# Expert routing done pass by pass inside the main loop of a decoder layer, with feed-forward tiles loaded by address

## The chip, the cores and the metric

The kernel runs on one core of a Trainium2 chip. A core has the engines PE (TensorE: matrix products and transposes), DVE (VectorE), ACT (ScalarE), POOL (GpSimd) and SP (SyncE, which here only starts transfers), each with a queue of instructions of its own that is worked in order; they wait for each other by semaphores. The time is the device time of one execution in microseconds (us); lower is better.

## What is computed

The input x is 32 sequences of 128 tokens with 128 features. Three pre-normalised residual blocks follow each other: self attention that keeps the 32 largest scores of each row, cross attention with 16 heads of 8, and a feed-forward stage with 8 experts (128 to 512 to 128), of which each token uses one. The part that the change is about, cut from the reference:

```python
aff = feats @ centroids.T              # feats: 4096 tokens x 128, layernorm of x
eid = jnp.argmax(aff, axis=1)          # the expert of each token
xhat = (feats - mu) * jax.lax.rsqrt(var + EPS)
for e in range(E):
    mask = (eid == e)[:, None]
    h = xhat * gamma[e] + beta[e]
    y = feats + jax.nn.relu(h @ w1[e] + b1[e]) @ w2[e] + b2[e]
    alpha = jax.nn.sigmoid(feats @ centroids[e])[:, None]
    out = out + mask * (alpha * y + (1.0 - alpha) * feats)
x = x + out
```

## The kernel before

**Main loop.** The 32 sequences go in 8 groups (NG = 8) of 4 (G = 4). `passes` runs `run(g)` for g from -3 to 8 on every engine. Pass g does the cross attention of group g (`has_c`, g from 0 to 7), the second half of the self attention of group e = g + 2 (`has_e`), the first half of that of group h = g + 3 (`has_s`) and the features of group f = g - 1 (`has_f`), so that passes 1 to 4 carry all four, pass 5 has no h, passes 6 and 7 have neither e nor h, and pass 8 has only the features of group 7. Each pass is eight steps. The order inside a pass is written out by hand for each engine. DVE takes the maxima of the cross scores (`next_maxima`, L836; then `hmax_split`, L849 and L851), which PE transposes (L1266) before the scores can be shifted, exponentiated on ACT (L1058) and multiplied with the values (L1278). Between the maxima DVE does the normalisation of the heads (L858, L863), layernorm statistics (L607, L612, L614), the top-32 search (L824 MAX8, L828) and small steps of the features: `aff` is copied from PSUM (L995), its maximum taken (L1013), then 1/(1+exp(-max)) made (L1024, L1030).

POOL adds the attention result to the residual (`add_attended`, L695, on which DVE's statistics of the features wait), masks queries (L689), makes the reciprocal roots (L618, L775) and applies the norms (L622, L626), and makes the payload of a group, `pay`: per token 128 normalised features, 128 of x2 + feats, alpha (L779, L794), 260 words of 4 bytes in all. SP stores it to DRAM in token order (L585), one transfer of 520 KB per group. In passes 6 and 7 POOL also scales the first weights of 8 experts (`scale_w1`, L710), each after a product of PE (`expert_bias`, L1442) whose result DVE adds (L885).

**Routing.** After the last pass `route_vector` (L302 to L367) works on the affinities of all 4096 tokens at once: one-hot of the best expert, counts by two products of PE (L396, L397), a running sum, a slot for each token, and then the inverse of that map: ACT (L500, L504) and DVE (L350) build one-hot matrices, and 32 products of PE (L407) turn them into `gather_idx` and `scatter_idx`, a token number for each place of 39 tiles of 128 rows (each expert's tokens fill whole tiles).

**Feed-forward.** For each of the 39 tiles POOL gathers 128 rows of `pay` by an indirect transfer (L524) into a ring of RING = 6 buffers and scatters the result to the output by another (L528). PE transposes the tile (L421), multiplies with w1 of the tile's expert (L429) and w2 (L440); ACT copies the transposed rows (L481), copies w1 (L487) and takes relu (L493); DVE adds biases (L455, L463) and makes the result (L469). In POOL's queue the gather of tile t stands behind the wait for the result of tile t - 6, and the scatter of t - 6 behind that gather. The tile's expert number is read into a register by `expert_of` on PE, DVE and ACT.

## Time and profile before

| | us |
|---|---|
| median of 3 runs (485.59 to 493.64) | 487.68 |
| the profiled execution | 489.07 |
| its span, first to last instruction | 486.9 |
| PE busy | 376.5 |
| DVE busy | 310.1 |
| POOL busy | 253.6 |
| ACT busy | 238.3 |

The profile shows the execution that took 489.07 us; 2.2 us of it lie outside the span. Starts in the trace count from the start of the span. The span has three stretches: the main loop up to about 348 us, the routing up to 373 us, and the tiles up to the last scatter at 478 us, behind which only its landing and the end of the program lie. The chain that ended last has only that one transfer in it and so says nothing of the stretches; they are read from the instructions in order of time.

### The profile page before, as it was taken

What the parts mean: (1) busy time and instruction counts of PE and PEld (TensorE: products, weight loads), DVE (VectorE), ACT (ScalarE), POOL (GpSimd) and SP (SyncE); (2) the same over time, 40 slices, a digit from 0 to 9 for tenths busy, and PEclk for the clock granted to TensorE, in tenths of its full rate; (3) what the DMA queues carried; (4) which work ended last, traced back from release to release, by engine and by line L of the source; (5) the groups of instructions that cost most, each with busy time, mean ns of one, the idle gap of its engine ahead of it and who ended that gap; (6) DMA issues with size and microseconds to landing.
All of it is one profiled execution on the core that took longest, in us unless ns stands there. A gap on an engine that the chain in (4) does not pass through costs nothing. (4 is left out here: it accounts for less than half of the span.)

```text
span 486.9 us, 10893 instructions
## 1 busy us (share of the span) xinstructions
PE 376.5 (77%) x3453; PEld 245.1 (50%) x3454; DVE 310.1 (64%) x1194; ACT 238.3 (49%) x497; POOL 253.6 (52%) x319
## 2 busy tenths in 40 slices
PE   1757778978988988889898989897204988888870
PEld 1435424544544545545544545454204878778770
DVE  2376946697897897887878464452493545555550
ACT  1143613657666566666665534342043655555540
POOL 6933550135663863764647434444404477777771
PEclk9996955999999999999999799997555899999996
DMA  5010107500003001020011000100202132222220
GB/s 133 24 44 0 46 0 224 165 3 22 2 2 88 2 21 48 3 67 2 1 46 46 25 21 2 45 1 7 83 1 55 45 82 70 73 76 69 71 64 0
DMA packets 23949, 21.67 MB, mean 45 GB/s; under 512 B 3443, under 2 KB 20983, under 8 KB 23904
## 3 DMA queue, kind: packets, MB, share of 16 engines
q1 hardware_dynamic: 19488, 13.52, 9.3%
q0 software_dynamic: 3120, 7.30, 5.5%
q8 instruction: 25, 0.41, 0.4%
q10 hardware_dynamic: 1296, 0.28, 0.3%
q14 instruction: 20, 0.16, 0.1%
HBM read 14.73 MB, written 6.82 MB: 44 GB/s over the span
## 5 line engine op out<-in xcount | busy, mean ns | idle before, releaser
L836 DVE TENSOR_REDUCE neg_hmax<-s_bank 128x4 f32<-128x512 f32 x128 | 82.2, 684 | 49.8 <-PE s_bank L1242 49.5
L1058 ACT ACTIVATE weights<-s_bank 128x512 f32<-128x512 f32 x128 | 69.5, 595 | 70.3 <-PE s_bank L1258 64.1
L1242 PE MATMUL s_bank<-k_room,q_room 32*128 32x512 f32 x256 | 83.8, 669 | 3.2 <-DVE neg_hmax L836 3.2
L695 POOL TENSOR_TENSOR x<-x_bv,attended 128x128 f32<-128x128 f32 x32 | 14.6, 457 | 121.3 <-DVE attended L863 121.3
L1253 PE MATMUL s_bank<-q_room,k_room 32*128 32x512 f32 x256 | 73.9, 654 | 0.0
L524 POOL DMA_INDIRECT q_room<-routed_rows,gather_idx x39 | 38.2, 979 | 38.4 <-DVE scatter_idx L361 22.8
L1278 PE MATMUL pvt_bank<-weights,xv 128*32 128x128 f32 x1024 | 49.8, 288 | 10.3 <-ACT weights L1058 8.6
L455 DVE TENSOR_TENSOR q_room<-s_bank,b_cols 128x512 f32<-128x512 f32 x39 | 27.0, 691 | 41.5 <-PE s_bank L429 41.5
L528 POOL DMA_INDIRECT out<-x_in,scatter_idx x39 | 39.5, 1012 | 15.8 <-issue 12.5
L429 PE MATMUL s_bank<-k_room,self_room 128*128 128x128 f32 x312 | 44.5, 287 | 0.0
L1278 PEld LDWEIGHTS pvt_bank<-weights,xv 128*32 128x32 f32 x1024 | 21.7, 110 | 44.0 <-ACT weights L1058 40.5
L618 POOL TENSOR_TENSOR rstd<-var_eps,minus_half 128x4 f32<-128x4 f32 x24 | 24.4, 1018 | 32.2 <-DVE var_eps L614 31.5
L429 PEld LDWEIGHTS s_bank<-k_room,self_room 128*128 128x128 f32 x312 | 39.7, 199 | 0.4
L487 ACT ACTIVATE self_room<-w 128x512 f32 x39 | 24.6, 630 | 28.7 <-PE s_bank L429 23.9
L1258 PEld LDWEIGHTS s_bank<-hmax_t,head_sel 32*128 32x128 bf16 x512 | 20.4, 94 | 30.0 <-issue 28.5
L828 DVE MATCH_REPLACE8 self_room<-best,self_room 128x128 f32<-128x128 f32 x128 | 33.8, 274 | 0.0
L824 DVE MAX8 best<-self_room 128x8 f32<-128x128 f32 x128 | 27.6, 277 | 9.5 <-ACT self_room L1049 9.5
L493 ACT ACTIVATE q_room<-q_room 128x512 f32<-128x512 f32 x39 | 24.6, 630 | 12.5 <-DVE q_room L455 10.2
L1242 PEld LDWEIGHTS s_bank<-k_room,q_room 32*128 32x128 f32 x256 | 24.4, 190 | 9.4 <-issue 5.1
L421 PE MATMUL cross_bank<-ident,q_room 128*128 128x128 f32 x39 | 12.7, 326 | 18.5 <-DMA q_room<-routed_rows,gather_idx 18.4
L689 POOL TENSOR_SCALAR q_room<-q_room,head_mask 128x512 f32<-128x512 f32 x32 | 22.2, 695 | 8.3 <-ACT q_room L1051 8.3
L1258 PE MATMUL s_bank<-hmax_t,head_sel 32*128 32x128 bf16 x512 | 26.1, 218 | 0.0
(183 smaller groups left out, 783.8 us busy)
## 6 DMA issues: line engine op xcount, KB each, us to landing
routed_rows<-pay SPq DMA_DIRECT2D x8, 520.0 KB, 3.3
w<-in_w SPq DMA_DIRECT2D x16, 256.0 KB, 5.2
x_in<-in_x SPq DMA_DIRECT2D x8, 256.0 KB, 3.1
ctx_in<-in_ctx SPq DMA_DIRECT2D x8, 256.0 KB, 3.3
q_room<-routed_rows,gather_idx POOLq DMA_INDIRECT x39, 2.8
out<-x_in,scatter_idx POOLq DMA_INDIRECT x39, 2.3
x_in<-in_b SPq DMA_DIRECT2D x1, 512.0 KB, 4.8
xwk_t<-in_xwk_t ACTq DMA_DIRECT2D x1, 64.0 KB, 2.8
```

Source lines behind the costliest of these rows:

```text
L429: m = pe.matmul(s1_bank[:, (k % 2) * F + c * 128:(k % 2) * F + (c + 1) * 128], ffn_w1[k % 2][:, c * 128:(c + 1) * 128], ffn_row_t[k % 2], ...
L455: dve.tensor_tensor(by_chunk(ffn_hid[k % 2]), by_chunk(s1_bank[:, (k % 2) * F:(k % 2 + 1) * F]), spread(at(b1_cols, e * FC, FC).rearrange( ...
L524: pool.indirect_dma_start(out=ffn_row[k], out_offset=None, in_=rows, in_offset=bass.IndirectOffsetOnAxis(ap=gather_idx[:, t:t + 1].bitcast ...
L528: pool.indirect_dma_start(out=out_rows, out_offset=bass.IndirectOffsetOnAxis(ap=scatter_idx[:, old:old + 1].bitcast(U32), axis=0), in_=ffn ...
L824: dve.max(best8[:, b, r, :], at(src, b * S, S)).then_inc(s["topk_step"], 1)
L828: dve.match_replace(at(left, b * S, S), best8[:, b, r, :], at(src, b * S, S), TAKEN)\
L836: dve.tensor_reduce(neg_hmax[:, first:first + 4], bank.rearrange("p (h k) -> p h k", k=S), AX.X, ALU.max, negate=True).then_inc(s["s1_max" ...
L1058: act.activation(weights[:, u, :], s2_bank[:, (u % 2) * GS:(u % 2 + 1) * GS], ACT.Exp, scale=HEAD_SCALE).then_inc(s["s2_exp"], 1)
L1242: pe.matmul(s1_bank[:, (u % 2) * GS:(u % 2 + 1) * GS], natural(q_nat, g, j, strip(u)), masked(k_masked, g, j, strip(u)), start=True, stop= ...
L1253: pe.matmul(s2_bank[:, (u % 2) * GS:(u % 2 + 1) * GS], natural(k_nat, g, j, u), masked(q_masked, g, j, u), start=True, stop=False)
L1258: m = pe.matmul(s2_bank[:, (u % 2) * GS + i * S:(u % 2) * GS + (i + 1) * S], head_sel[32 * u:32 * (u + 1), i, :], hmax_t[32 * u:32 * (u + ...
L1278: m = pe.matmul(pvt_bank[32 * i:32 * (i + 1), (u % 2) * S:(u % 2 + 1) * S], xv[:, block:block + 32], weights[:, u, i * S:(i + 1) * S], sta ...
```

## The change

The routing is split over the passes. One pass after the affinities of a group, DVE marks the best expert of each token (`best_marked`, `best_ranked`, `first_best`: 4 operations of 128x32), PE counts (`count_rows`: 5 small bf16 products into a free part of `att_bank`), DVE reads the counts (`read_counts`) and makes a row number for each token (`slots`: 5 operations). Each expert has an area of its own in DRAM of CAP = 4224 rows, and POOL scatters the payload of a group straight into the areas (`scatter_rows`: 4 indirect transfers of 128 rows, 133 KB each), at four places of the pass for groups 0 to 5 (in pass f + 2), and all four behind each other at the end of pass f + 1 for groups 6 and 7. The payload gets two buffers and a token number in each row. SP's store of the payload is gone.

At the end `route_vector` only works out how many tiles each expert has and the first row of each tile (15 operations: 11 of 8 to 39 columns, 4 of 312). SP and ACT write a blank of 128 rows behind the end of each area (`blank_tails`, 8 transfers of 133 KB); the token number of a blank row is out of range, so that its result is not stored. SP then loads the 39 tiles with plain transfers at an address read from `tile_row` into a register (`ffn_sync`), up to eight ahead (RING = 8). POOL keeps only the scatter of the results, by the token numbers in the loaded rows. The products of L396, L397 and L407 and ACT's L500 and L504 are gone. `q_masked` is a ring of 2 in place of 3; POOL's wait for it then asks for the cross scores of group g - 1 in pass g.

```diff
-    NTC = NTILE + 1
+    CAP = B * S + 128
     PAY = 2 * D + 4
+    ALPHA, TOKEN = 2 * D, 2 * D + 1
+    NOWHERE = 1 << 20
...
-    RING = 6
-
-    rows = nc.dram_tensor("routed_rows", [B * S, PAY], F32, kind="Internal").ap()
+    RING = 8
+
+    rows = nc.dram_tensor("routed_rows", [E * CAP + 128, PAY], F32, kind="Internal").ap()
     out_rows = out.rearrange("b s d -> (b s) d")
...
+        Q_RING, K_RING = 2, 3
+        q_room = sb("q_room", [128, Q_RING * MASKED + 3 * GS])
+        k_room = sb("k_room", [128, K_RING * MASKED + 3 * GS])
+        q_masked, k_masked = q_room[:, 0:Q_RING * MASKED], k_room[:, 0:K_RING * MASKED]
+        q_nat, k_nat = q_room[:, Q_RING * MASKED:], k_room[:, K_RING * MASKED:]
...
+        def routed_at_once(f):
+
+            return f >= NG - 2
+
+        def routed_later(f):
+
+            return 0 <= f < NG - 2
...
+            dve.wait_ge(s["next_row_ready"], 1 + NG)
+            link(dve.tensor_scalar(next_row_i[:, :], next_row[:, :], 0.0, None, ALU.add))
+            s_ends = dve.tensor_scalar(first_f[:, 0:E], next_row[:, :], 127.0, None, ALU.add)
+            s_ends.then_inc(s["ends_ready"], 1)
+            dve.wait_ge(s["ends_ready"], 1)
+            link(dve.tensor_copy(tiles_i[:, :], first_f[:, 0:E]))
+            link(dve.tensor_scalar(tiles_i[:, :], tiles_i[:, :], 7, None, ALU.logical_shift_right))
+            link(dve.tensor_copy(tiles_of[:, :], tiles_i[:, :]))
+            link(dve.scalar_tensor_tensor(tiles_of[:, :], iota_f[:, 0:E], float(-CAP // 128), tiles_of[:, :], ALU.mult, ALU.add))
+            link(dve.tensor_tensor_scan(tiles_end[:, :], ones_f[:, :], tiles_of[:, :], 0.0, ALU.mult, ALU.add))
+            link(dve.tensor_scalar(jump[:, :], tiles_of[:, :], -128.0, float(CAP), ALU.mult, ALU.add))
+            link(dve.tensor_tensor(after[:, :, :], spread(col(iota_f[:, 0:NTILE]), [128, NTILE, E]),
+                                   spread(row(tiles_end[:, :]), [128, NTILE, E]), ALU.is_ge))
+            link(dve.tensor_reduce(expert_f[:, :], after[:, :, :], AX.X, ALU.add))
+            dve.tensor_scalar(tile_expert[:, :], expert_f[:, :], float(E - 1), None, ALU.min).then_inc(s["experts_ready"], 1)
+            link(dve.tensor_tensor(after[:, :, :], after[:, :, :], spread(row(jump[:, :]), [128, NTILE, E]), ALU.mult))
+            link(dve.tensor_reduce(first_f[:, :], after[:, :, :], AX.X, ALU.add))
+            link(dve.scalar_tensor_tensor(first_f[:, :], iota_f[:, 0:NTILE], 128.0, first_f[:, :], ALU.mult, ALU.add))
+            dve.tensor_scalar(tile_row[:, :], first_f[:, :], float(E * CAP), None, ALU.min).then_inc(s["tile_rows_ready"], 1)
             dve.wait_ge(s["experts_ready"], 1)
             ffn_vector(dve)
...
+            for t in range(NTILE):
+                k = t % RING
+                pool.wait_ge(s["result_ready"], t + 1)
+                pool.indirect_dma_start(out=out_rows,
+                                        out_offset=bass.IndirectOffsetOnAxis(ap=ffn_row[k][:, TOKEN:TOKEN + 1].bitcast(U32), axis=0),
+                                        in_=ffn_out[k], in_offset=None, bounds_check=B * S - 1,
+                                        oob_is_err=False).then_inc(row_scattered[k], 16)
             for k in range(RING):
                 n = len(range(k, NTILE, RING))
                 wait_alone(pool, row_scattered[k], 16 * n)
+
+        def blank_tails(eng, experts):
+            wait_alone(eng, s["route_step"], 1)
+            for e in experts:
+                end = eng.value_load(next_row_i[0:1, e:e + 1], min_val=0, max_val=E * CAP)
+                eng.dma_start(rows[ds(end, 128), :], blank[:, :]).then_inc(s["blanks_stored"], 16)
+
+        def ffn_sync(sp):
+            blank_tails(sp, range(0, E // 2))
+            wait_alone(sp, s["blanks_stored"], 16 * (1 + E))
+            for i in range(2):
+                wait_alone(sp, pay_stored[i], 16 * G * NG // 2)
+            wait_alone(sp, s["s2_done"], 4 * B)
+            wait_alone(sp, s["tile_rows_ready"], 1)
+            for t in range(NTILE):
+                k = t % RING
+                if t >= RING:
+                    wait_alone(sp, row_scattered[k], 16 * (t // RING))
+                first = sp.value_load(tile_row[0:1, t:t + 1], min_val=0, max_val=E * CAP)
+                sp.dma_start(ffn_row[k], rows[ds(first, 128), :]).then_inc(row_loaded[k], 16)
...
-                if has_f:
-                    wait_alone(sp, s["pay_ready"], g)
-                    wait_alone(sp, s["alpha_ready"], g)
-                    sp.dma_start(rows[ds((g - 1) * GS, GS), :].rearrange("(b s) c -> s b c", s=S),
-                                 pay[:, :, :]).then_inc(s["pay_stored"], 16)
...
+            def scatter_rows(f, j):
+
+                if j == 0:
+                    wait_alone(pool, s["pay_ready"], f + 1)
+                    wait_alone(pool, s["tokens_ready"], f + 1)
+                    wait_alone(pool, s["alpha_ready"], f + 1)
+                    wait_alone(pool, s["slots_ready"], f + 1)
+                at0 = half(f) * G + j
+                pool.indirect_dma_start(out=rows, out_offset=bass.IndirectOffsetOnAxis(ap=slot[:, at0:at0 + 1].bitcast(U32), axis=0),
+                                        in_=pay[:, at0, :], in_offset=None, bounds_check=E * CAP - 1,
+                                        oob_is_err=False).then_inc(pay_stored[half(f)], 16)
...
                         norm_apply(pool, 2, f, at(x2, half(f) * GS, GS), centred[:, :], feats[:, :], "feats_ready")
+                if routed_later(f - 1):
+                    scatter_rows(f - 1, 0)
...
+                    pool.iota(pay_of(f)[:, :, TOKEN].bitcast(I32), pattern=[[S, G]], base=f * GS, channel_multiplier=1)\
+                        .then_inc(s["tokens_ready"], 1)
+                if routed_later(f - 1):
+                    scatter_rows(f - 1, 3)
+                if has_f and routed_at_once(f):
+                    for j in range(G):
+                        scatter_rows(f, j)
...
+            def best_marked(f):
+
+                dve.wait_ge(s["aff_max_ready"], f + 1)
+                dve.tensor_tensor(chosen[:, :, :], aff[:, :, :], spread(col(aff_max[:, :]), [128, G, E]), ALU.is_equal)\
+                   .then_inc(s["chosen_step"], 1)
+
+            def best_ranked(f):
+
+                dve.wait_ge(s["chosen_step"], 3 * f + 1)
+                dve.tensor_tensor(chosen[:, :, :], chosen[:, :, :], spread(row(rank[:, :]), [128, G, E]), ALU.mult)\
+                   .then_inc(s["chosen_step"], 1)
+
+            def first_best(f):
+
+                dve.wait_ge(s["chosen_step"], 3 * f + 2)
+                dve.tensor_reduce(best[:, :], chosen[:, :, :], AX.X, ALU.max).then_inc(s["chosen_step"], 1)
+                dve.wait_ge(s["chosen_step"], 3 * f + 3)
+                dve.tensor_tensor(onehot[:, 0:G, :], chosen[:, :, :], spread(col(best[:, :]), [128, G, E]), ALU.is_equal)\
+                   .then_inc(s["onehot_ready"], 1)
+
+            def read_counts(f):
+
+                dve.wait_ge(s["counts_done"], f + 1)
+                dve.tensor_copy(counts[:, :, :], att_bank[:, COUNTS:COUNTS + (G + 1) * E].rearrange("p (b e) -> p b e", e=E))\
+                   .then_inc(s["counts_read"], 1)
+
+            def slots(f):
+
+                dve.wait_ge(s["counts_read"], f + 1)
+                dve.wait_ge(s["next_row_ready"], f + 1)
+                dve.tensor_tensor(placed[:, :, :], counts[:, 0:G, :], spread(row(next_row[:, :]), [128, G, E]), ALU.add)\
+                   .then_inc(s["placed_step"], 1)
+                dve.wait_ge(s["placed_step"], 3 * f + 1)
+                dve.tensor_tensor(next_row[:, :], next_row[:, :], counts[:, G, :], ALU.add).then_inc(s["next_row_ready"], 1)
+                dve.tensor_tensor(placed[:, :, :], placed[:, :, :], onehot[:, 0:G, :], ALU.mult).then_inc(s["placed_step"], 1)
+                dve.wait_ge(s["placed_step"], 3 * f + 2)
+                dve.tensor_reduce(slot_f[:, :], placed[:, :, :], AX.X, ALU.add).then_inc(s["placed_step"], 1)
+                if later(f, 2):
+                    dve.wait_ge(pay_stored[half(f)], 16 * G * (f // 2))
+                dve.wait_ge(s["placed_step"], 3 * f + 3)
+                dve.tensor_copy(slot[:, half(f) * G:(half(f) + 1) * G], slot_f[:, :]).then_inc(s["slots_ready"], 1)
...
                     next_maxima(g, 0, 2)
+                if routed_later(f - 1):
+                    read_counts(f - 1)
...
                 expert_bias(g, 0)
+                if routed_later(f - 1):
+                    slots(f - 1)
...
+                    best_marked(f)
                 if has_s:
-                    topk(h, 2)
+                    topk_best(h, 2)
+                if has_f:
+                    best_ranked(f)
+                if has_s:
+                    topk_take(h, 2)
+                if has_f:
+                    first_best(f)
 
                 if has_c:
                     next_maxima(g, 3, 2)
                 if has_s:
                     topk(h, 3)
+                if has_f and routed_at_once(f):
+                    read_counts(f)
+                    slots(f)
...
+                if j == 0 and routed_later(g - 2):
+                    pe.wait_ge(s["counts_read"], g - 1)
+                if j == 3 and routed_at_once(g - 1):
+                    pe.wait_ge(s["counts_read"], g)
...
+                def count_rows(of):
+                    pe.wait_ge(s["onehot_ready"], of + 1)
+                    pe.wait_ge(s["iota_made"], 5)
+                    pe.wait_ge(s["attended_ready"], G * (of + 2) if routed_later(of) else min(G * of + 7, B))
+                    pe.matmul(att_bank[:, COUNTS:COUNTS + (G + 1) * E], earlier[:, :],
+                              onehot[:, :, :].rearrange("p b e -> p (b e)"), start=True, stop=False)
+                    for b in range(G):
+                        m = pe.matmul(att_bank[:, COUNTS + (b + 1) * E:COUNTS + (G + 1) * E], all_ones[:, :],
+                                      spread(onehot[:, b:b + 1, :], [128, G - b, E]), start=False, stop=b == G - 1)
+                    m.then_inc(s["counts_done"], 1)
...
                         transposed(lambda b: xn[:, b * S:(b + 1) * S], self_bank, h, "xn_ready", h + 1, "xn_transposed")
+                    if routed_later(f - 1):
+                        count_rows(f - 1)
...
                         project(cross_bank, xwq_t, xn2_t, "xn2_t_ready", e + 1, "xq_done")
+                    if routed_at_once(f):
+                        count_rows(f)
```

## Rows read from the trace of the kernel before

**Rows 1.** Busy time by window: start:end, length, PE, PEld, DVE, ACT, POOL, PE's clock, DMA.
```profile
207.10:240.60 33.50, 30.09 (x336) 17.09 (x336) 28.53 (x119) 21.28 (x46) 19.99 (x25) 1.00 0.09 25
...
373.00:380.00 7.00, 6.31 (x28) 6.00 (x29) 1.38 (x2) 3.76 (x8) 3.33 (x4) 0.50 0.34 94
```
**Rows 2.** DVE in time, passes 4 and 5: start, us, line, operation, [idle before].
```profile
223.98 1.29 DVE L836 TENSOR_REDUCE neg_hmax<-s_bank 128x4 f32<-128x512 f32 x2 [0.81 <-PE s_bank L1242]
...
255.87 1.28 DVE L836 TENSOR_REDUCE neg_hmax<-s_bank 128x4 f32<-128x512 f32 x2
```
**Rows 3.** PE and its weight loads in time, start of pass 4.
```profile
217.61 0.10 PEld L1266 LDWEIGHTS s_bank<-ident_bf,hmax_parts 128*128 128x128 bf16 x1 [1.44 <-DVE hmax_parts L851]
...
220.02 0.66 PE L1217 MATMUL self_bank<-ident,self_room 128*128 128x128 f32 x4
```
**Rows 4.** POOL in time, between passes 3 and 4.
```profile
214.89 1.04 POOL L626 TENSOR_TENSOR self_room<-centred,rstd 128x512 f32<-128x512 f32 x1
218.13 0.46 POOL L695 TENSOR_TENSOR x<-x_bv,attended 128x128 f32<-128x128 f32 x1 [2.20 <-DVE attended L863]
```
**Rows 5.** Timeline: two DVE operations, and the POOL instruction beside each.
```profile
199.84 1.04 POOL L626 TENSOR_TENSOR xn<-centred,rstd 128x512 f32<-128x512 f32 x1
200.00 0.92 DVE L849 CAST hmax_parts<-neg_hmax 128x16 bf16<-128x16 f32 x1
...
369.74 1.24 POOL L524 DMA_INDIRECT q_room<-routed_rows,gather_idx  x1 [22.77 <-DVE scatter_idx L361]
370.10 0.18 DVE L366 TENSOR_SCALAR k_room<-k_room 128x40 f32<-128x40 f32 x1
```
**Rows 6.** Timeline of the last two passes.
```profile
338.66 1.04 POOL L794 TENSOR_TENSOR pay<-feats,rstd 128x512 f32<-128x512 f32 x1
339.66 0.45 POOL L695 TENSOR_TENSOR x<-x_bv,attended 128x128 f32<-128x128 f32 x1
...
347.62 0.19 DVE L995 COPY aff<-att_bank 128x32 f32<-128x32 f32 x1 [3.77 <-PE att_bank L1416]
```
**Rows 7.** Timeline of the routing.
```profile
352.43 0.40 PE L396 MATMUL s_bank<-k_room,earlier 128*128 128x256 bf16 x1 [4.85 <-DVE k_room L311]
...
353.08 0.69 DVE L313 COPY k_room<-s_bank 128x512 f32<-128x512 f32 x1 [0.70 <-PE s_bank L397]
...
356.32 0.17 DVE L325 TENSOR_TENSOR k_room<-k_room 128x8 f32<-128x8 f32 x1
356.52 0.17 DVE L326 SCALAR_TENSOR_TENSOR k_room<-k_room 128x8 f32<-128x8 f32 x1
...
369.06 0.48 DVE L363 TENSOR_TENSOR k_room<-iota_f,k_room 128x320 f32<-128x320 f32 x1
```
**Rows 8.** PE's tile transposes in time: tiles 0, 3, 6 and 38.
```profile
372.95 0.45 PE L421 MATMUL cross_bank<-ident,q_room 128*128 128x128 f32 x1 [5.06 <-DMA q_room<-routed_rows,gather_idx]
...
379.79 0.42 PE L421 MATMUL cross_bank<-ident,q_room 128*128 128x128 f32 x1
...
385.81 0.27 PE L421 MATMUL cross_bank<-ident,q_room 128*128 128x128 f32 x1
...
470.08 0.33 PE L421 MATMUL cross_bank<-ident,q_room 128*128 128x128 f32 x1 [0.58 <-DMA q_room<-routed_rows,gather_idx]
```
**Rows 9.** POOL's steady pace in the tiles, in time.
```profile
427.35 0.98 POOL L524 DMA_INDIRECT q_room<-routed_rows,gather_idx  x1 [0.30 <-issue]
...
428.63 1.01 POOL L528 DMA_INDIRECT out<-x_in,scatter_idx  x1 [0.30 <-issue]
```
**Rows 10.** The page, part 6: transfers, us from issue to landing.
```profile
q_room<-routed_rows,gather_idx POOLq DMA_INDIRECT x39, 2.8
out<-x_in,scatter_idx POOLq DMA_INDIRECT x39, 2.3
```
**Rows 11.** Timeline: a start by SP; ACT's copy of w1 behind a register read.
```profile
2.76 0.43 SPq L551 DMA_DIRECT2D bias_cols<-in_bk  x1
...
374.08 0.63 ACT L487 ACTIVATE self_room<-w 128x512 f32 x1 [0.37 <-issue]
```

269 lines of the change are left out of this document (83 added, 186 removed).

## The prediction

> **What bounds the kernel now.** I read the page first, then the busy time by window, then the waits, and last each stretch in order of time. The chain of waits on the page ends in one scatter and does not help, so each stretch has to be judged by itself.
>
> In the main loop a full pass takes 33.5 us, of which PE is busy 30.1, DVE 28.5 and POOL 20.0 [rows 1]. DVE has 119 instructions in it, and behind most a gap of some 0.04 us, 4 to 5 us in all, so DVE has nearly no idle time left. PE and DVE take turns: at one place PE waits 1.44 us for the split maxima [rows 3], at another DVE waits 0.81 us for PE's scores, and at the same place a pass later it waits for nothing [rows 2]. An operation added to DVE therefore costs between nothing and its whole length, by its place. POOL has 13 us to spare, mostly in waits for DVE; one of them is 2.20 us [rows 4].
>
> The routing lies bare: from the last copy of the affinities at 347.62 [rows 6] to the first transpose of a tile at 372.95 [rows 8] it takes 25.3 us, and neither PE nor POOL has other work.
>
> In the tiles two paces stand beside each other. POOL spends 0.98 + 0.30 + 1.01 + 0.30 = 2.59 us per tile on a gather and a scatter [rows 9]. PE, where it did not wait for rows, went from tile 3 to tile 6 in 385.81 - 379.79 = 6.02 us, 2.01 us per tile [rows 8]. The stage as a whole went from tile 3 to tile 38 in 90.3 us, 2.58 us per tile, so POOL sets it. The first three intervals are an exception: PE then had a granted clock of 0.50, the level of 1.2 GHz [rows 1], behind a stretch in which it had been nearly idle, and needed 379.79 - 372.95 = 6.84 us for them.
>
> **The change, part by part.**
>
> *Tiles.* POOL loses the gather and comes down to 1.01 + 0.30 = 1.31 us per tile. PE is next, at 2.01 us; I take 2.04, a little over it, because the three intervals are few. SP's own pace is not in the trace: a start took it 0.43 us, and a register read on ACT showed as at most 0.37 us of idle time before L487 [rows 11]. With a wait in front I estimate 1 us per tile, and up to eight tiles of lead. Its bounds are 0.43 us, the bare start, and 2.59 us, the nearest loop of starts and waits that there is [rows 9]; above 2.04 it would show. ACT and DVE kept up with the 2.01. A row load takes about what a gather took to land, 2.8 us [rows 10], against a lead of 8 x 2.04 = 16 us. So tiles 0 to 3 take 6.84 us as before, tiles 3 to 38 35 x 2.04 = 71.4, together 78.2 in place of 470.08 - 372.95 = 97.1: **-18.9 us**. What follows tile 38 stays, 486.9 - 470.08 = 16.8.
>
> *From the last affinities to the first tile.* Small dependent operations of DVE follow each other by 356.52 - 356.32 = 0.20 us [rows 7]. From the copy of `aff`: the maximum and four marking operations end at 0.2 + 5 x 0.2 = 1.25. The old counts took 353.08 - 352.43 = 0.65 us from PE's start to DVE's read [rows 7]; five products of at most 40 columns are taken the same, 1.9. `read_counts` and the five of `slots` make 3.1, two for alpha 3.5. Then three things run beside each other. (1) POOL issues four scatters: 1.24 for a first indirect transfer [rows 5], then 3 x 1.31, the last landing 2.3 us behind its start, at about 3.5 + 1.24 + 2.6 + 0.3 + 2.3 = 9.9. (2) DVE's end of the routing: 11 operations by 0.20 and four of 312 columns by 0.52 (0.48 [rows 7] and a gap), 4.3, ready at 7.8. (3) `next_row_i` at 3.7; SP and ACT then write four blanks each, a register read and a start, 0.43 to 1.2 us each, so that the last starts between 5 and 8.5 and lands some 3 later, at 8 to 11.5; I take 10.6. Then a register read, a start and 2.8 us of landing, 3.6 to 3.9: the first transpose at **14.5** in place of 25.3, a gain of 10.8 us; the bounds are 12 and 18.
>
> *POOL's queue at the end of pass 7.* Here the moved work falls on the path. Before, POOL ended `pay` (L794) at 339.70 and at 339.66 began the last addition to the residual (L695) [rows 6], on which the last group's statistics, its features and its affinities hang. The operand of that addition had come at 338.95. Now the token numbers (about 0.2), `scatter_rows(5, 3)` and the four of group 6 stand between the two: 5 x 1.28, by (0.98 + 0.30) of [rows 9], is 6.4. What waits is L695, and with it everything to the last affinities: **+6.6 us**, bounds 5 and 8. So little of the routing gain is left: 10.8 - 6.6 = **-4.2 us** at the start of the tiles.
>
> *Main loop.* DVE: four marking operations, two of them between independent ones, some 0.65 us, in passes 1 to 4 in a place where PE later waits for DVE [rows 3]: on the path, 4 x 0.65 = 2.6. `read_counts` and `slots`, six operations, 1.2 us, in passes 2 to 5, before the L836 that once had 0.81 us of idle time and once none [rows 2]: 0.7 each, 2.8. Passes 5 to 7 have less DVE work; five products of PE (0.3 to 0.6 us) in each cost a little there, together 0.1. Sum **+5.5 us**, bounds 1 (all hidden) and 12 (7 passes x (0.65 + 1.2) uncovered, less 1).
>
> POOL: four scatters by 1.28, 5.1 us per pass, into 13 us of idle time. The worst place is the end of a pass: two scatters and the token numbers, 2.7 us, ahead of `first_norm`, whose end at 215.93 [rows 4] goes to 218.6. PE takes those rows at 220.02 [rows 3], and the addition behind had 2.20 us of idle time. Hidden, by 1.4 us; that much more POOL time in this place would reach PE, and DVE's `read_counts` behind it.
>
> SP's store of 520 KB goes; its landing was hidden. The q ring of two asks for scores that POOL's own wait for the last head result already implies: nothing. At the start POOL loses three small constants and gains four: nothing.
>
> *Two engines at one memory.* A cast of 16 columns (L849) took 0.92 us, not about 0.17, beside an arithmetic instruction of POOL; L366 beside an indirect transfer on POOL took 0.18 [rows 5]. So I give the scatters no price on DVE. The Trainium skill, SBUF — State Buffer, section "Who interferes with whom", says that VectorE's two-port modes and GpSimd exclude each other for the whole instruction, whoever issues first, and that descriptor making suffers by this too. By that rule the cast of this trace is explained, and the scatters would meet DVE operations as well, which the pair with L366 does not show.
>
> **The sum.** -18.9 - 10.8 + 6.6 + 5.5 = -17.6 us. On the profiled execution 489.07 - 17.6 = 471.5. That execution lies 1.4 us above the median of 487.68, so for the median: 487.7 - 17.6 = **470 us**, 3.6% less.
>
> **The rivals.**
>
> 1. *The small work is hidden and the path at pass 7 is shorter.* Main loop +1 and the start at 12 in place of 14.5: 470 - 4.5 - 2.5 = 463; with POOL's stop at 5 us, 461. For it: passes 5 to 7 wait often on PE. Against: the places where PE waits for DVE.
> 2. *The tiles stop at another bound.* SP's wait, register read and start, or a chain over ACT and DVE, at 2.3 to 2.4 us per tile: 35 x 0.33 = 11.5 more, 481.5, within 2%. For it: SP's pace was never seen, and PE's was seen only on a few tiles. Against: [rows 11].
> 3. *The scatters disturb the loop.* If 24 scatters of groups 0 to 5 each hold DVE or are held as the cast was, 0.92 - 0.17 = 0.75 us, that is 18 us: 488, no change. The rule of the Trainium skill above, SBUF — State Buffer, goes this way. Half of it gives 479. Against: L366.
> 4. *Slower.* SP's loads come at a pace P. The forecast turns to a loss of over 2% (above 497.4) when 35 x (P - 2.04) passes 27.4 us, at P = 2.82 us per tile; at 3.0 the time is 504. Against it: even POOL, with two indirect transfers, needs 2.59.
>
> **How the numbers follow.** Forecast as told (465 to 476) 0.47, rival 1 0.15, rival 2 0.16, rival 3 0.14 (half of it near 479, half near 488), rival 4 0.05, other 0.03. About 2% is what a measurement of this kernel can tell from no change; faster means below 477.9. Faster: 0.47 + 0.15, a third of rivals 2 and 3, 0.72. Same: the rest of these, 0.21. Slower: rival 4, a little of the other, 0.07. The range reaches from rival 1 to rival 2 with half of rival 3: 459 to 485.
>
> **What would show it.** In the changed kernel: L421's successor every 2.0 to 2.1 us with clock 1.00 and no wait for a load behind the first; POOL busy about half of the tile stage; five indirect transfers in a row on POOL before the last L695, which starts 6 to 7 us behind L794's successor; 14 to 15 us from the last copy of `aff` to the first transpose; full passes 1 to 1.5 us longer; small DVE casts of 0.17 us beside scatters. The prediction is wrong if tiles come at over 2.2 us, if passes grow by over 2.5 us, or if L695 does not wait for the scatters.

## The result, and the profile after

| us | before | after |
|---|---|---|
| median of 20 runs each | 486.86 (484.99 to 493.64) | 483.22 (482.12 to 488.1) |
| the profiled execution, its span | 489.07, 486.9 | 483.1, 481.3 |
| PE, DVE, POOL, ACT busy | 376.5, 310.1, 253.6, 238.3 | 380.5, 318.9, 249.6, 229.7 |

The ratio of the runs is 0.995, with a 95% interval of 0.9932 to 0.9967. The change is worth 3.6 us where 17.6 were forecast. By the two spans it is 5.6 us; the profiled execution of before lay over the median of its kernel and that of after on it, which makes the other 2 us. In one group of experiments (the first section on them) the runs of before stood at 516.7 us, far from the 486 to 487 of all the other groups; no trace of such a run was kept, and the reason is open. The changed kernel was not timed in that group, so its kernels are set against the changed kernel's 483.0 to 483.2 of the others.

The span falls into the same stretches as before. Each difference below is between two rows of the same kind, of [rows 6] and [rows 8] for before and of the fences for after.

| stretch | before | after | difference | forecast |
|---|---|---|---|---|
| start to the end of the pass-7 payload (POOL) | 339.7 | 354.0 | +14.3 | +5.5 |
| from there to the last addition to the residual | 0.0 | 6.5 | +6.5 | +6.6 |
| last addition to the last copy of the affinities | 8.0 | 8.0 | 0.0 | 0 |
| last affinities to the first tile transpose | 25.3 | 14.8 | -10.5 | -10.8 |
| first to last tile transpose | 97.1 | 81.8 | -15.3 | -18.9 |
| last transpose to the end of the span | 16.8 | 16.2 | -0.6 | 0 |

The busy time by window of the kernel after (start:end, length, then PE, PEld, DVE, ACT, POOL, PE's clock, DMA share, GB/s). The first three are passes 1, 2 and 3, cut at the copies of `aff`; the last two are the tiles:

```profile
138.69:175.61 36.92, 32.75 (x341) 18.65 (x341) 30.94 (x138) 21.60 (x47) 22.01 (x28) 0.95 0.05 16
175.61:212.06 36.45, 33.06 (x341) 17.96 (x341) 32.08 (x139) 21.49 (x47) 24.64 (x31) 0.95 0.07 24
212.06:249.40 37.34, 32.97 (x341) 18.30 (x341) 31.77 (x130) 21.60 (x47) 24.62 (x31) 0.95 0.07 23
383.00:390.00 7.00, 6.08 (x27) 5.81 (x28) 1.38 (x2) 3.76 (x8) 0.00 (x0) 0.50 0.44 116
390.00:465.00 75.00, 72.80 (x596) 68.95 (x595) 46.48 (x105) 49.28 (x104) 32.98 (x35) 1.00 0.31 84
```

Cut in the same way, the three passes of before take 34.1, 34.1 and 33.7 us, so they grew by 2.8, 2.3 and 3.6; PE's mean clock in them is 0.95 and not 1.00. From the first copy of `aff` to that of pass 7 the loop took 189.7 us before and takes 203.5 after. A second profile of the changed kernel (`after_again`) has 206.9 there, so a difference of 3 us between two profiled loops is within what one kernel shows. In the tiles PE is busy 97% of the time at clock 1.00, and POOL 44%.

The end of pass 7 on POOL, and the last copy of `aff`, in order of time (start, us, engine, line, operation, [idle before]):

```profile
352.97 1.04 POOL L740 TENSOR_TENSOR pay<-feats,rstd 128x512 f32<-128x512 f32 x1
353.96 0.14 POOL L743 IOTA pay<- 128x4 int32 x1
354.26 1.07 POOL L634 DMA_INDIRECT routed_rows<-pay,slot  x1 [0.16 <-issue]
...
359.49 0.98 POOL L634 DMA_INDIRECT routed_rows<-pay,slot  x1 [0.30 <-issue]
360.49 0.47 POOL L623 TENSOR_TENSOR x<-x_bv,attended 128x128 f32<-128x128 f32 x1
...
368.48 0.19 DVE L1009 COPY aff<-att_bank 128x32 f32<-128x32 f32 x1 [3.77 <-PE att_bank L1445]
```

Five indirect transfers stand between the payload and the addition (L623, L695 before), as forecast: 360.49 - 354.0 = 6.5 us.

The start of the tiles: SP's four blanks, the last scatter, SP's first load, and the transposes of tiles 0, 3 and 38 on PE:

```profile
372.73 4.36 SPq L447 DMA_DIRECT2D routed_rows<-blank  x4
...
376.58 0.97 POOL L634 DMA_INDIRECT routed_rows<-pay,slot  x1 [0.30 <-issue]
...
381.16 0.36 SPq L461 DMA_DIRECT2D q_room<-routed_rows  x1
...
383.30 0.45 PE L351 MATMUL cross_bank<-ident,q_room 128*128 128x128 f32 x1 [13.15 <-DMA q_room<-routed_rows]
...
390.05 0.31 PE L351 MATMUL cross_bank<-ident,q_room 128*128 128x128 f32 x1
...
465.12 0.27 PE L351 MATMUL cross_bank<-ident,q_room 128*128 128x128 f32 x1
```

What SP waits for ahead of its first load is the last scatter, not the blanks, which have no row among the waits of SP (us in total, times, longest):

```profile
SPq L214 <- DMA routed_rows<-pay,slot: 3.2, 1, 3.2
```

### The profile page after: what moved, and what is told of

Read it like the earlier page. It is cut to its first block and busy times, and to the rows that moved or that the text cites. A ratio compares the mean times of both kernels' runs of the same rounds, so it can differ in the third digit from the quotient of the medians.

```text
span 481.3 us, 11235 instructions
## 1 busy us (share of the span) xinstructions
PE 380.5 (79%) x3459; PEld 245.8 (51%) x3460; DVE 318.9 (66%) x1248; ACT 229.7 (48%) x479; POOL 249.6 (52%) x321
## 5 line engine op out<-in xcount | busy, mean ns | idle before, releaser
L1265 PE MATMUL s_bank<-k_room,q_room 32*128 32x512 f32 x256 | 87.5, 683 | 4.7 <-DVE neg_hmax L795 4.7
L1276 PE MATMUL s_bank<-q_room,k_room 32*128 32x512 f32 x256 | 75.9, 671 | 0.0
L623 POOL TENSOR_TENSOR x<-x_bv,attended 128x128 f32<-128x128 f32 x32 | 14.5, 454 | 109.1 <-DVE attended L822 109.1
L435 POOL DMA_INDIRECT out<-x_in,q_room x39 | 37.7, 967 | 58.5 <-DVE x_in L399 57.8
L359 PE MATMUL s_bank<-k_room,self_room 128*128 128x128 f32 x312 | 43.1, 283 | 0.0
L634 POOL DMA_INDIRECT routed_rows<-pay,slot x32 | 34.4, 1074 | 11.3 <-issue 6.6
L787 DVE MATCH_REPLACE8 self_room<-best,self_room 128x128 f32<-128x128 f32 x128 | 33.7, 273 | 0.0
L1265 PEld LDWEIGHTS s_bank<-k_room,q_room 32*128 32x128 f32 x256 | 25.7, 194 | 14.8 <-DVE neg_hmax L795 9.5
L1276 PEld LDWEIGHTS s_bank<-q_room,k_room 32*128 32x128 f32 x256 | 20.4, 193 | 12.6 <-issue 8.5
```

What stands on the lines that cost most here:

```text
L359: m = pe.matmul(s1_bank[:, (k % 2) * F + c * 128:(k % 2) * F + (c + 1) * 128], ffn_w1[k % 2][:, c * 128:(c + 1) * 128], ffn_row_t[k % 2], ...
L435: pool.indirect_dma_start(out=out_rows, out_offset=bass.IndirectOffsetOnAxis(ap=ffn_row[k][:, TOKEN:TOKEN + 1].bitcast(U32), axis=0), in_= ...
L634: pool.indirect_dma_start(out=rows, out_offset=bass.IndirectOffsetOnAxis(ap=slot[:, at0:at0 + 1].bitcast(U32), axis=0), in_=pay[:, at0, :] ...
L787: dve.match_replace(at(left, b * S, S), best8[:, b, r, :], at(src, b * S, S), TAKEN)\
L1265: pe.matmul(s1_bank[:, (u % 2) * GS:(u % 2 + 1) * GS], natural(q_nat, g, j, strip(u)), masked(k_masked, K_RING, g, j, strip(u)), start=Tru ...
L1276: pe.matmul(s2_bank[:, (u % 2) * GS:(u % 2 + 1) * GS], natural(k_nat, g, j, u), masked(q_masked, Q_RING, g, j, u), start=True, stop=False)
```

## Experiments

Two kinds of difference are used. Against the changed kernel it is between medians. Against the kernel before, timed beside each experiment, it is the ratio of the runs, with its 95% interval, times the median of before.

The first group (`late_scatters`, `chosen_in_psum`, `tiles_unrolled`, `all_three`) was timed on a chip on which the changed kernel itself was not, so its gains rest on the changed kernel's 483.0 us of the other groups. What the traces can say of this supports it: from tile 3 to tile 38 the two kernels of this group that keep the loop over the tiles take 74.9 and 75.0 us, `after_again` 74.9, `scatters_behind_norm` 75.0 and the changed kernel 75.1, and the two with the tiles written out in this group take 70.1 each, like `all_four` of another.

### One part of the changed kernel at a time

**The scatters of the last pass behind the last addition** (`late_scatters`).

```
                     add_attended(f, 3)
+                if f == NG - 1:
+                    scatter_rows(NG - 3, 3)
...
-                if routed_later(f - 1):
+                if routed_later(f - 1) and f - 1 != NG - 3:
                     scatter_rows(f - 1, 3)
-                if has_f and routed_at_once(f):
-                    for j in range(G):
-                        scatter_rows(f, j)
+                if has_f and f == NG - 1:
+                    for late in (NG - 2, NG - 1):
+                        for j in range(G):
+                            scatter_rows(late, j)
```

> The changed kernel with five scatters moved in POOL's queue: scatter_rows(5, 3) stands behind the last addition to the residual (L623 of the changed kernel), and the four of group 6 stand with those of group 7 at the end of pass 8. Theory A (they stood on the path): the last L623 starts where pay and token numbers end, 6.4 us earlier, everything behind it too, and 3 to 6 us of that reach the end, since POOL now has eight scatters in a row when the last slots come (about 1.5 us too late for the last four): about 478 us. Rival (what waits ahead of L623 is DVE's last head result or a product of PE, and the scatters only fill that gap): under 1 us gained, 483.

It took 478.25 us (476.85 to 481.28), 4.8 less than the changed kernel; between the two profiled executions, of which this one was the fastest of its four, the span fell by 6.2. POOL of this kernel in order of time:

```profile
353.88 0.14 POOL L745 IOTA pay<- 128x4 int32 x1
353.99 0.45 POOL L623 TENSOR_TENSOR x<-x_bv,attended 128x128 f32<-128x128 f32 x1
...
361.60 1.07 POOL L634 DMA_INDIRECT routed_rows<-pay,slot  x1 [0.17 <-issue]
...
370.65 0.97 POOL L634 DMA_INDIRECT routed_rows<-pay,slot  x1 [0.31 <-issue]
```

The addition begins right behind the payload, at 353.99 and not at 360.49. Eight scatters now stand in a row at the end, but the first four run while the last group's results are still on their way, and the last of the eight starts 5.9 us earlier than in the changed kernel (370.65 against 376.58). The cost of the queue place is shown, and it was avoidable.

**The marks in PSUM** (`chosen_in_psum`). For groups 0 to 3 the operand `chosen` of the marking operations lies in a free part of PSUM; PE waits for `onehot_ready` before it writes there again.

```
+            def chosen_of(f):
+                if f < 4:
+                    return self_bank[:, 0:G * E].rearrange("p (b e) -> p b e", e=E)
+                return chosen[:, :, :]
...
-                dve.tensor_tensor(onehot[:, 0:G, :], chosen[:, :, :], spread(col(best[:, :]), [128, G, E]), ALU.is_equal)\
+                dve.tensor_tensor(onehot[:, 0:G, :], chosen_of(f), spread(col(best[:, :]), [128, G, E]), ALU.is_equal)\
```

The reason for it is a place in passes 2, 3 and 4 of the changed kernel. Here it is in pass 3, DVE and POOL, in order of time:

```profile
216.76 0.17 DVE L857 TENSOR_REDUCE best<-chosen 128x4 f32<-128x32 f32 x1
216.88 1.28 POOL L735 TENSOR_TENSOR x_bv<-x,xbv_rows 128x512 f32<-128x512 f32 x1
216.97 2.24 DVE L859 TENSOR_TENSOR onehot<-chosen,best 128x32 bf16<-128x32 f32 x1
218.11 1.04 POOL L740 TENSOR_TENSOR pay<-feats,rstd 128x512 f32<-128x512 f32 x1
219.10 0.14 POOL L743 IOTA pay<- 128x4 int32 x1
219.13 0.68 DVE L795 TENSOR_REDUCE neg_hmax<-s_bank 128x4 f32<-128x512 f32 x1
```

L859 handles 32 columns and has a median of 0.19 us over its eight executions, but it takes 2.24 here, over the whole of two arithmetic instructions of POOL that follow each other, and ends as they do. In pass 1 the operation L851 (two SBUF operands too) takes 1.19 us in place of 0.17, beside L735 alone: it ends as L740 begins.

> The changed kernel with the tile chosen in PSUM (self_bank, free at that time) for groups 0 to 3, so that L851, L857 and L859 read at most one operand from SBUF; the same operations in the same places. Theory B (a DVE operation with two SBUF operands stands still while POOL's tensor_tensor instructions read SBUF, 2.05 us in each of passes 2, 3 and 4 at L859 and 1.02 us in pass 1 at L851): L859 takes 0.2 us in every pass, passes 1 to 4 get shorter by 1 to 2 us each, the three stretches with PE at 0.50 of its clock in passes 1 to 3 disappear, and the time falls by 5 to 8 us, to 476 to 478. Rival B1 (the long L859 is DVE's own time for writing bf16 or waiting for the scatter L634): L859 stays at 2.2 us and the time at 483. Rival B2 (L859 gets short but the passes are bound elsewhere): under 2 us gained.

It took 479.05 us (478.55 to 481.58), 4.0 less than the changed kernel. The same pair of instructions in this kernel:

```profile
218.88 1.27 POOL L735 TENSOR_TENSOR x_bv<-x,xbv_rows 128x512 f32<-128x512 f32 x1
218.97 0.19 DVE L864 TENSOR_TENSOR onehot<-self_bank,best 128x32 bf16<-128x32 f32 x1
```

With one operand in PSUM it takes 0.19 us beside the same work of POOL. So what held it was its two operands in SBUF beside POOL's instructions, and not its size or a wait. L851 takes 0.18 in pass 1 as well. The three stalls of 2.05 us and that one of 1.02 make 7.2, of which 4.0 came back, under the 5 to 8 that I had expected. Two things are left. PE's stretches at half clock did not all go, as I had expected of them: its mean clock in passes 1, 2 and 3 is 0.95, 0.91 and 1.00. And pass 2 did not get shorter but longer, 38.8 us for 36.5, since PE waits 4.34 us in it for the split maxima; the reason is shown below, with `psum_and_norm`.

**The tiles written out** (`tiles_unrolled`). The loop over rounds of eight tiles is unrolled; the work on the data is the same.

```
-            for t in range(first, RING):
-                step(t // RING, t % RING)
-            with eng.Fori(1, NTILE // RING) as i:
-                for r in range(RING):
-                    step(i, r)
-            for t in range(NTILE // RING * RING, last):
+            for t in range(first, last):
                 step(t // RING, t % RING)
```

> The changed kernel with the 39 feed-forward tiles written out instead of a loop over rounds of eight buffers. Theory C (the long steps between tile transposes, 2.4 to 2.55 us twice in each round of eight, and 2.08 to 2.18 inside it, are the loop's jump and its register arithmetic): 2.02 to 2.05 us per tile from tile 3 to tile 38 in place of 2.145, 3 to 4 us gained, 479 to 480. Rival (PE is bound by its own products and by waits for relu on ACT): no change, 483.

It took 478.18 us (477.33 to 480.25), 4.8 less. From tile 3 to tile 38 PE needs 70.1 us, 2.00 per tile, where the changed kernel needs 465.12 - 390.05 = 75.1, 2.145 per tile. Transposes of five tiles that follow each other in the changed kernel, in time:

```profile
424.00 0.27 PE L351 MATMUL cross_bank<-ident,q_room 128*128 128x128 f32 x1
...
426.55 0.27 PE L351 MATMUL cross_bank<-ident,q_room 128*128 128x128 f32 x1
...
428.94 0.27 PE L351 MATMUL cross_bank<-ident,q_room 128*128 128x128 f32 x1
...
431.02 0.27 PE L351 MATMUL cross_bank<-ident,q_room 128*128 128x128 f32 x1
...
433.11 0.27 PE L351 MATMUL cross_bank<-ident,q_room 128*128 128x128 f32 x1
```

At each turn of the loop two steps are long, here 2.55 and 2.39 us; between the turns they are some 2.1. The window in the kernel written out:

```profile
392.00:462.00 70.00, 69.46 (x596) 67.99 (x595) 46.31 (x105) 49.15 (x104) 32.88 (x34) 1.00 0.34 91
```

PE is idle for 0.5 us of 70, against 2.2 of 75 with the loop. The loop was taken out of PE, DVE and ACT at once, so the engine whose turn costs is not shown: in the changed kernel PE waits in the two long steps, 0.40 and 0.23 us, for a result of ACT. How much of the loop's cost is its turn and how much the addresses made in registers was not separated either.

**All three together** (`all_three`).

> The three changes above together: scatters of groups 5 and 6 late, chosen in PSUM, tiles written out. If each theory holds and they add, 483 - 5 - 6.5 - 3.5 = 468 us (465 to 471). If A and B overlap (the earlier end of the loop brings the same POOL queue to the last slots), 471 to 474. If only the rivals hold, 483.

It took 470.0 us (468.51 to 470.5): 13.0 less than the changed kernel, where the three parts alone make 4.8 + 4.0 + 4.8 = 13.6. They lie in different stretches and add up.

### Parts of the change added to the kernel before

These three do the routing of before in full and add unused work, so that nothing is won back elsewhere.

**The marks alone** (`before_with_marks`): the ten DVE operations and five PE products per group at the places that they have in the change, for the groups up to 6 (of group 7 only the four marking operations); the results are not used.

```
+                if has_f:
+                    best_marked(f)
                 if has_s:
-                    topk(h, 2)
+                    topk(h, 2, (lambda: best_ranked(f)) if has_f else None)
...
+                    if routed_later(f - 1):
+                        count_rows(f - 1)
```

> The kernel before, with the change's marking and slot operations on DVE (ten per pass) and its five counting products on PE put at the same places of passes 1 to 7; nothing uses their results, routing and tiles stay as before, and POOL has no scatters. Theory B (the price of the main loop is paid on DVE: work plus standing still beside POOL): +6 to +12 us on before, 493 to 499, with L859's counterpart at over 0.5 us in some passes. My forecast's own price for this part was +5.5. Rival D (the price comes from the scatters): under +3.

It took 494.25 us, the ratio to before is 1.0165 (1.0106 to 1.0223), 8.0 us (5.2 to 10.8). The marks stand still beside POOL here too, but elsewhere: the second of them in passes 1 to 4, for 1.20 us, beside one POOL instruction, and the last one (L859 of the changed kernel) not at all in these passes. In pass 3:

```profile
214.03 1.20 DVE L914 TENSOR_TENSOR chosen_n<-chosen_n,rank 128x32 f32<-128x32 f32 x1
...
216.41 0.19 DVE L921 TENSOR_TENSOR onehot_n<-chosen_n,best_n 128x32 bf16<-128x32 f32 x1
```

**The scatters alone** (`before_with_scatters`): 24 indirect transfers of one row of zeros per partition into spare DRAM, four in each of passes 2 to 7, at the places of `scatter_rows`, without any DVE or PE work.

```
+            def spare_rows(g, j):
...
+                n = 4 * (g - 2) + j
+                pool.indirect_dma_start(out=spare, out_offset=bass.IndirectOffsetOnAxis(ap=spare_idx[:, n:n + 1].bitcast(U32), axis=0),
+                                        in_=spare_row[:, :], in_offset=None, bounds_check=24 * 128 - 1,
+                                        oob_is_err=False).then_inc(s["spare_stored"], 16)
```

> The kernel before, with 24 more indirect transfers of 128 rows of 1040 bytes from a tile of zeros to a spare DRAM tensor, four in each of passes 2 to 7 at the places of the change's scatters; nothing else changed, and no marking on DVE. Theory B: POOL has room, only the one at the end of pass 7 stands ahead of the last addition to the residual: +1.3 us, at most +3. Rival D (scatters disturb the loop): +6 or more.

It took 497.0 us, 1.0196 (1.013 to 1.0262), 9.5 us, where I had expected nothing. The end of pass 2 of this kernel, in order of time:

```profile
180.55 1.02 POOL L711 DMA_INDIRECT spare<-spare_row,spare_idx  x1 [0.17 <-issue]
181.59 1.06 POOL L623 TENSOR_TENSOR rstd<-var_eps,minus_half 128x4 f32<-128x4 f32 x1
182.62 1.04 POOL L627 TENSOR_TENSOR centred<-x_in,moments 128x512 f32<-128x512 f32 x1
183.76 0.87 DVE L612 BATCH_NORM_STATS2 stats<-x_in 128x6 f32<-128x128 f32 x4 [2.98 <-POOL centred L627]
186.86 0.29 PE L1287 MATMUL s_bank<-ident_bf,hmax_parts 128*128 128x128 bf16 x1 [4.22 <-DVE hmax_parts L872]
186.94 2.02 PE L1370 MATMUL cross_bank<-xwv_t,ctx_t 128*128 128x128 f32 x8
```

Read it downward. The scatters stand in POOL's queue ahead of `first_norm`, so `centred` comes later. DVE's statistics of the next group lead to the buffer `moments`, which `centred` reads, and so wait for it, 2.98 us. Behind them in DVE's queue are the cross maxima, so PE waits 4.22 us for the split maxima, where in before it waits 1.60 at this place of this pass. The last row shows a second loss: eight products take 2.02 us, at the start of a stretch of about 7 us with a granted clock of 0.50. In the kernel `before_scat_behind` (below), at clock 1.00, the same eight take 1.11:

```profile
183.35 1.11 PE L1375 MATMUL cross_bank<-xwv_t,ctx_t 128*128 128x128 f32 x8
```

**Both** (`before_with_both`).

> The two additions together on the kernel before. If DVE's operations stand still longer because the scatters push POOL's tensor_tensor instructions under them (L859's counterpart at 2.2 us in passes 2 to 4, which needs both), the sum is larger than its parts, by 3 to 6 us; if the parts are independent, it is their sum. The changed kernel's own loop was 14.3 us longer than before up to the end of pass 7's payload.

It took 505.36 us, 1.0364 (1.0302 to 1.0426), 17.7 us; the parts make 1.65% + 1.96% = 3.6%. So the times add up, and the sum is not 3 to 6 us larger. The stall that was to make it larger is there all the same: in passes 2 to 4 the last marking operation takes 2.23 to 2.24 us, which it does with neither part alone. In pass 3:

```profile
218.68 2.23 DVE L942 TENSOR_TENSOR onehot_n<-chosen_n,best_n 128x32 bf16<-128x32 f32 x1
```

The scatter ahead pushes POOL's arithmetic from the second mark onto the last one. In return the statistics' wait of 2.98 us for `centred`, which the scatters alone had brought, is gone: DVE comes to that place late by its own stall. One loss took the other's place. From the first `aff` to that of pass 7, by the profiled executions, the marks cost 5.0 us, the scatters 9.2, both 14.6; the changed kernel stands 13.8 over before, and its second profile 17.2. As far as such single profiles can tell, this is the main loop of the change, rebuilt in before.

### What of a scatter costs: its place, its bytes

**Scatters 2 and 3 behind the norm, in before** (`before_scat_behind`) and **the same bytes by SP** (`before_stores_by_sp`). The first is `before_with_scatters` with the last two scatters of passes 2 and 3 moved behind `first_norm(h + 1)`. The second writes the 24 x 133 KB with plain transfers of SP, and POOL has none of it.

```
                     first_norm(h + 1)
+                if isinstance(g, int) and g in (2, 3):
+                    spare_rows(g, 2)
+                    spare_rows(g, 3)
```

```
...
+                    for j in range(4):
+                        wait_alone(sp, s["attended_ready"], G * g + j)
+                        n = 4 * (g - 2) + j
+                        sp.dma_start(spare[n * 128:(n + 1) * 128, :], spare_row[:, :]).then_inc(s["spare_stored"], 16)
```

> The kernel before with the 24 spare scatters, of which the third and fourth of passes 2 and 3 stand behind first_norm in POOL's queue. With them in front the price was 10 us (497.0 against 486.1). Theory E: DVE's 2.98 us of waiting for the centred of the next group in pass 3, and the half-clock stretch of PE behind it, are gone: +3 to +7 in place of +10, 489 to 493. Rival (the place does not matter, the scatters cost by their number): 496 to 497.

> The kernel before with 24 more transfers of 128 rows of 1040 bytes into a spare DRAM tensor in passes 2 to 7, as plain transfers started by SP, none by POOL. Theory E (the price is POOL's time in its queue and beside DVE): at most +1 us, 486 to 487. Rival (the bytes and the DMA engines are the price): +6 or more.

The first took 490.53 us, 1.0091 (1.0061 to 1.0121), 4.4 us in place of 9.5 (by the medians alone 3.6 in place of 10.9); the second 485.03, 0.998 (0.9958 to 1.0002), no cost at all. So the bytes cost nothing, and half of the scatters' cost or somewhat more is the place of four of them, ahead of `first_norm` in two passes. In the first kernel DVE's statistics of the same place follow without a wait:

```profile
180.19 0.86 DVE L612 BATCH_NORM_STATS2 stats<-x_in 128x6 f32<-128x128 f32 x4
```

Of the other 4.4 us, paid by the 20 scatters whose place was kept, the traces show where and not why: cut at the copies of `aff`, pass 5 takes 32.0 us here, 29.7 in before and 27.7 with the stores by SP, at mean granted clocks of 0.86, 0.91 and 1.00. Whether POOL's time or the clock is the cause stays open.

**The same move in the changed kernel** (`scatters_behind_norm`, and with the marks in PSUM `psum_and_norm`); the changed kernel itself was timed again beside them (`after_again`).

```
-                if routed_later(f - 1):
+                if routed_later(f - 1) and h + 1 >= NG:
                     scatter_rows(f - 1, 2)
...
-                if routed_later(f - 1):
+                if routed_later(f - 1) and h + 1 >= NG:
                     scatter_rows(f - 1, 3)
...
                     first_norm(h + 1)
+                    if routed_later(f - 1):
+                        scatter_rows(f - 1, 2)
+                        scatter_rows(f - 1, 3)
```

> The changed kernel unchanged, as the mark for the others of this call: 0.995 of before, about 483 us.

> The changed kernel with the third and fourth scatter of passes 2 and 3 behind first_norm in POOL's queue, so that L547, for which DVE's statistics of the next group wait (L532), comes 2.5 us earlier. Theory E (two stalls stand side by side at the end of a pass: DVE's standing still at L859, and DVE's wait for L547 behind the scatters; taking one away lays the other bare): alone it brings under 2 us, since L859 still stands still: 481 to 483. Rival (the scatters are the price of the loop, as 9.5 us on the kernel before suggests): 5 us or more, 478.

> The move of the scatters behind first_norm together with chosen in PSUM. Theory E: both stalls are gone, no idle time at L532 in pass 3 (it was 2.00 us with chosen in PSUM alone), and the time is 1.5 to 4 us under chosen in PSUM alone (479.05), about 476.5. Rival (the rest of the price is DVE's own ten operations and PE's clock): no further gain, 479.

`after_again` took 483.01 us, 0.9942 (0.9923 to 0.9961) of before. The move gave 479.64, 0.987 (0.9844 to 0.9897), 3.4 less than `after_again`, more than I had expected; both together 477.84, 0.9844 (0.9816 to 0.9871), 5.2 less, where 3.4 and the 4.0 of the marks in PSUM would make 7.4, and only 1.2 under `chosen_in_psum`, where I had expected 1.5 to 4.

The two don't add up, and my reason for the move was only half of it. I had taken the stall of L859 to stay where it was. But one of the two scatters that are moved stood ahead of the POOL arithmetic that causes it. With it gone from there the last marking operation is free in passes 2 and 3 (in pass 4, whose scatters were not moved, it still takes 2.23), and the second one takes 1.21 in its stead. In pass 3 of `scatters_behind_norm`:

```profile
212.69 1.26 POOL L735 TENSOR_TENSOR x_bv<-x,xbv_rows 128x512 f32<-128x512 f32 x1
212.79 1.21 DVE L854 TENSOR_TENSOR chosen<-chosen,rank 128x32 f32<-128x32 f32 x1
213.91 1.03 POOL L740 TENSOR_TENSOR pay<-feats,rstd 128x512 f32<-128x512 f32 x1
...
215.17 0.19 DVE L862 TENSOR_TENSOR onehot<-chosen,best 128x32 bf16<-128x32 f32 x1
```

So both edits take away parts of one stall. The other half of my reason holds: in the changed kernel the statistics' wait for `centred` is hidden behind the stall of L859, and it comes to light when that stall alone is gone. In `chosen_in_psum`, DVE at the end of pass 2:

```profile
185.86 0.87 DVE L532 BATCH_NORM_STATS2 stats<-x_in 128x6 f32<-128x128 f32 x4 [2.00 <-POOL centred L547]
```

With both edits this wait has no row.

**All four** (`all_four`): late scatters, marks in PSUM, tiles written out, scatters behind the norm.

> Late scatters of groups 5 and 6, chosen in PSUM, tiles written out, and the scatters of passes 2 and 3 behind first_norm. Three of them gave 470.0 us. Theory E: 466 to 468.5. Rival: 470.

It took 467.41 us (465.51 to 468.24), 0.961 (0.9583 to 0.9636) of before: 15.6 less than the changed kernel and 18.7 less than before. I had expected 466 to 468.5. It is the fastest version of the study.

## Why the prediction was wrong in size and right in direction

The time lies between 459 and 485, but the change is worth a fifth of what was forecast, and it is "same" by 2% where "faster" had 0.72. The range itself was drawn loosely: the numbers that it names, rival 1 and rival 2 with half of rival 3, make 461 and 490, not 459 and 485. In the span's sum 12.0 us are missing: the main loop cost 8.8 more than forecast and the tiles gave 3.6 less; the other steps together came out 0.4 better.

**Tiles: mechanism right, size off.** POOL's pace was the bound and PE's became it; SP was never late behind the first loads, and its first start took 0.36 us and eight in a row 8.32, the 1 us each of the estimate. The term that was mis-sized is 2.04 us per tile: it measured 2.145. The term's source, the three intervals of [rows 8] at 2.01, lies in tiles 3 to 6, and the first RING tiles stand ahead of the register loop. I extended a pace of written-out code to a stage that is mostly a loop. `tiles_unrolled` runs at 2.00, so the figure was right for such code; its 4.8 us is the price of the loop (5.0 between the traces). Rival 2 named a bound at 2.3 to 2.4 us by SP, ACT or DVE, and none of them was it. In the kernel before, a loop's cost of this size would have been hidden under POOL's 2.59; that is argued and not tested.

**Last affinities to the first tile: the number right, partly by luck.** 14.8 us for 14.5. But SP waits last for the scatters (1), where I had taken the blanks (3) to be last: the last scatter starts 8.1 us behind the copy of `aff` and lands 4.6 later, not 2.3, so the rows were complete at 12.7 us and not at 10.6; and what followed, a start and its landing, took 2.1 us and not 3.6 to 3.9. The two errors, of about +2.1 and -1.8 us, cancel. The four blanks of SP took 4.36, 1.09 each.

**POOL's queue at the end of pass 7: right.** 6.5 us for 6.6. `late_scatters` undid it.

**Main loop: the step that failed** is the sentence "Hidden, by 1.4 us" with its paragraph, which gave POOL's four scatters per pass no price. The term "Main loop" stood at 5.5 us and measured 14.3, beyond its own bound of 12; two of the three full passes grew by over 2.5 us, which the prediction had named as a sign of being wrong. In before the scatters alone cost 9.5 us, and the marks alone 8.0 by the ratio of the runs (5.2 to 10.8) and 5.0 by the profiled passes (the profiled execution was the fastest of its four), so the 5.5 of the forecast is not ruled out for them. I had compared the late end of `first_norm` only with PE's use of its rows at 220.02 [rows 3]. There was a second reader of POOL's work in between: DVE's statistics of the next group may only start when `centred` is done, and they stand in DVE's queue ahead of the maxima for which PE waits. That wait is in the code (`ln0_centred`), and in the trace of before it showed nothing, because `centred` was then always done in time; a wait that is met leaves no row. In the changed kernel itself it leaves none either, and the late POOL work is paid there in another way, told in the next paragraph. That the place of these scatters costs in the changed kernel too is shown by `scatters_behind_norm`: 3.4 us.

**Two engines at one memory: the wrong pair was asked.** From [rows 5] I concluded that scatters cost DVE nothing beside them, and that held: beside the scatter at 215.73 the top-32 operations keep their 0.27 us. But the marks are themselves DVE operations with two operands in SBUF, put at a place where POOL does arithmetic, and the four were priced at 0.65 us together. One of them, L859, took 2.24 us in three passes, L851 took 1.19 in one, and L845, the first, has a median of 0.45 over its eight executions. With the marks alone in before the longest of them in full passes was 1.20; the 2.24 came only with the scatters, which push POOL's arithmetic under L859. The page of the Trainium skill that the prediction cites, SBUF — State Buffer, section "Who interferes with whom", also says that a VectorE instruction with two inputs in SBUF contends with a GpSimd instruction that reads SBUF. The trace agrees, with 2.24 us beside L735 and L740 and 0.19 us once an operand is in PSUM; I had used only the section's rule on two-port modes.

**Rival 3** had, with half of its 18 us, about the right cost, and the wrong cause. The scatters did disturb the loop, but for at least half of it by the place that they take in POOL's queue, and not by their traffic: 9.5 us at their place, 4.4 with four of them moved, none when SP writes the same bytes. DVE is not held beside a scatter itself in the rows looked at, but beside the arithmetic that the scatter puts off. **Rivals 1 and 4** did not happen.

**A cost that I had no term for** is PE's clock. In passes 1 to 3 of before, cut at the copies of `aff`, the granted clock is 1.00 and PE is busy 30.1 us in each; in the changed kernel the clock is 0.95 in each, with a stretch of about 3.4 us at 0.50 (1.2 GHz), and PE is busy 32.8 to 33.1 us. In `before_with_scatters` the stretch follows directly on PE's wait of 4.22 us, as the two rows there show, and eight products at that level cost 0.9 us more. The five small products account for 1.0 us of the longer busy time: in `scatters_behind_norm` the clock is 1.00 in all three passes and PE is busy 31.1.

What the stretch costs by itself can be read in pass 1, where `late_scatters`, `tiles_unrolled` and `scatters_behind_norm` have the same instructions as the changed kernel, and PE waits 2.13 us for the split maxima at the place where it waits 2.12 in the changed kernel. There the clock did not fall:

```profile
137.98:173.30 35.32, 31.14 (x341) 17.57 (x341) 30.96 (x139) 21.61 (x47) 22.04 (x28) 1.00 0.05 16
```

That is pass 1 of `late_scatters`; `tiles_unrolled` has 35.32 us too and `scatters_behind_norm` 35.31, and the two profiles of the changed kernel have 36.92 and 36.60, at 0.95. The 35.31 and the 36.60 (`after_again`) are from one chip. So the same work behind the same wait came with and without the stretch, and the stretch cost this pass 1.3 to 1.6 us; the other 1.2 us over the 34.14 of before are the marks and what they bring. In passes 2 and 3 waits and clock move together in these traces, and how much of the loop's 14 us is clock stays open. It also changes between executions of one kernel: the 20 runs of the changed kernel reach from 482.12 us at a mean granted clock of 0.912 to 488.1 at 0.892.

## What to carry to other kernels

Before work is put into the queue of an engine that seems to have time to spare, list every instruction of every other engine that waits for what stands behind it, in the code and not only in the trace, since a wait that is met today leaves no row, and look at which other engine's small operations the work behind it will then fall on. Before small DVE operations are placed, look at what POOL computes at that moment and count how many of the operands lie in SBUF. And take the pace of a stage from the part of it that has the same form (loop or written-out code) as the part that it is to stand for.
